# Routing weights stored to DRAM and read back as broadcast rows, in an AdaLN / RWKV / mixture-of-experts kernel

## The chip, the cores and the metric

One core of one Trainium2 chip. The metric is device microseconds of one execution, the median of three runs. TensorE is called PE here, VectorE DVE, ScalarE ACT, GpSimd POOL, and SyncE, which only issues DMAs, SP.

## The reference

`x` is 4 batches of 1024 rows of 256 floats. Cut to what matters:

```
mod = silu(c) @ wmod                      # shifts, scales and gates of each batch
h = layernorm(x) * (1 + ca) + sa
x = x + ga * attn(h)                      # RWKV: projections k, v, r; a scan over time; Wo
h = layernorm(x) * (1 + cb) + sb
logits = h @ gate_w.T                     # 8 experts
topk_vals, topk_idx = top_k(logits, 2);  w = softmax(topk_vals)
comb = zeros((n, 8)).at[rows, topk_idx].add(w)
y = einsum('ne,enh->nh', comb, silu(h @ Wg) * (h @ Wu) @ Wd)     # each expert is 64 wide
y = y + silu(h @ sWg) * (h @ sWu) @ sWd                           # shared expert, 128 wide
x = x + gb * y
```

## The kernel before, in words

The 4096 rows are cut into 8 chunks of 512. Feature data lie transposed: features on the 128 partitions, 512 rows along the free dimension. Software pipelining is written out by hand: each engine has its own function `step(n)` with a fixed order of calls (PE L867, DVE L1222, ACT L547), and in step n it handles four chunks: `before` = n-2 (output of the expert layer), `prev` = n-1 (expert layer), `cur` = n (end of the attention, second norm), `nxt` = n+1 (first norm, projections, scan); DVE also takes the first statistics of `after` = n+2. Steps 0 and 1 have functions of their own, and `step(n)` runs for n = 2 to 9. Steps 2 to 6 have all their chunks; step 7 has no `nxt`, step 8 no `cur`. An engine works through its list strictly in order, and semaphores join the lists.

The expert layer of `prev` in one step: `up(prev, 0..9)` (PE L749) makes the gate and up products of the shared expert (i = 0, 1) and of four expert pairs, six matmuls each. `silu(prev, e)` (ACT L439) waits for `up(2e)`, `gate_up(prev, e)` (DVE L1138) for `up(2e+1)`. `route` (DVE L1080, 19 small operations) makes the routing weights from the logits and writes them to `comb` as a float32r high part and a low part, 16 columns. `turn_comb` (PE L741) transposes them, `comb_out` (ACT L469) copies them to `combT`, and `spread_comb(prev, e)` (PE L789) multiplies `combT` by a selection matrix `sel`, so that a PSUM bank holds the weight of each row on all 64 partitions of its expert. `weigh(prev, e)` (DVE L1150) multiplies by it. `down(prev, oc)` (PE L799) waits for all four `weigh`s and runs 10 matmuls; it is called for oc = 0 and 1.

Beside it in the same step: `turn_attn(cur, k)` (PE L711) transposes the attention output back, `residual1(cur, k)` (DVE L1058) adds x, `stats2(cur)` (DVE L1156) takes its statistics, `rstd` (POOL L296) works out the scale, `normalise2(cur)` (ACT L340, line L331) normalises, and `turn2(cur, kc)` (PE L649, line L631) transposes the result, which waits for all of `normalise2`. `affine2(cur)` (ACT L363), `low_part(cur)` (DVE L1074) and the `up`s of the next step follow. `project(nxt, j)` (PE L659) are the six projections of the next chunk, four matmuls each.

ACT's list ahead of `normalise2(cur)` in each step is: `silu(prev, 4)`, a table load, four exponentials and eight `state_falls`/`output_falls`, `add_bias(nxt, 2)` and `add_bias(nxt, 3)` (L574 to L583).

The end of PE's list in `step(n)` before:

```
up(prev, 6); spread_comb(prev, 1); up(prev, 7); spread_comb(prev, 2)
up(prev, 8); up(prev, 9); spread_comb(prev, 3); spread_comb(prev, 4)
turn_attn(cur, 1); project(nxt, (2, 3, 4))
down(prev, 0); turn2(cur, 0); turn2(cur, 1); project(nxt, (5,)); down(prev, 1)
```

SP (L233) has one in-order list of DMAs: the inputs and weights, then in a loop `load(n + 3)` (waits for `residual1` of chunk n, since `x_in` has three buffers) and `store(n)` (waits for `residual2` of chunk n, which DVE runs in step n+2).

Of the kernel before, what the change touches and what calls it, by code (L numbers as in the profile page):

```python
# [45 lines left out]
def adaln_rwkv_moe(nc, x, Wk, bk, Wv, bv, Wr, br, Wo, bo, tmk, tmv, tmr, time_decay, time_first,  # L46
                   gate_w, Wg, Wu, Wd, sWg, sWu, sWd, cond, wmod, out):
    x_chunks = x.rearrange("b (g t p) h -> (b g) p t h", t=TT, p=P)
    out_chunks = out.rearrange("b (g t p) h -> (b g) p t h", t=TT, p=P)

    with ExitStack() as ctx:
        def sb(name, shape, dt=F32):
# [6 lines left out]
        ident = sb("ident", [P, P])  # L59
        sel = sb("sel", [P, NP, P], F32R)  # L60
        prio = sb("prio", [P, TT, E])
# [39 lines left out]
        r1 = sb("r1", [P, 7, TT])  # L101
        comb = sb("comb", [P, TT, 2 * E], F32R)
        combT = sb("combT", [P, CH], F32R)
        lgT = sb("lgT", [2 * E, CH])
# [14 lines left out]

        sel_f = tmp[0:2 * E, 0, :].rearrange("p (i n) -> p i n", i=NP)  # L120
        rec = arg[:, 0, :, :]
# [7 lines left out]

        comb_bank = {1: cb, 2: cb, 3: cb, 4: tp}  # L130

# [4 lines left out]
        class Norm:  # L136
# [21 lines left out]
            sem(n) for n in ("cond_in", "rows_in", "mod_in", "mod2_in", "up_in", "dn_in", "gw_in"))  # L158
        consts_done, ident_done, sel_done = sem("consts_done"), sem("ident_done"), sem("sel_done")
        zeros_done = sem("zeros_done")  # L160
        sq_in = [sem(f"sq_in{w}") for w in range(4)]
# [44 lines left out]
        combT_done = sem("combT_done")  # L206
        comb_mm = sem("comb_mm")
        up_mm = sem("up_mm")
# [11 lines left out]
        bias_cols = (col["bk"], col["bv"])  # L220
        ROUTE_STEPS = 18
        N_CONSTS2 = 4
# [10 lines left out]
        def _(sp):  # L233
# [28 lines left out]
            load(chunk(2))  # L262
            for n in range(NC - 1):
                if chunk(n + 3):
                    load(chunk(n + 3))
                store(chunk(n))
            last = chunk(NC - 1)
# [10 lines left out]
        def _(pool):  # L278
            nc.gpsimd.memset(ident[:, :], 0.0).then_inc(consts_done, 1)
            nc.gpsimd.memset(sel_f[:, :, :], 0.0).then_inc(consts_done, 1)  # L280
# [3 lines left out]
            pool.wait_ge(consts_done, 5)  # L284
# [3 lines left out]
            for part in range(2):  # L288
                wait(pool, sel_done, part)
                nc.gpsimd.affine_select(  # L290
                    out=sel_f[:, :, :].rearrange("p i (e m) -> p i e m", m=M),
                    in_=sel_f[:, :, :].rearrange("p i (e m) -> p i e m", m=M),
                    compare_op=ALU.not_equal, fill=1.0, base=-E * part,
                    pattern=[[-2, NP], [-1, 2], [0, M]], channel_multiplier=1).then_inc(sel_done, 1)

# [30 lines left out]
        def _(ac):  # L326
# [300 lines left out]
        def _(pe):  # L627
# [112 lines left out]
            @of_chunk  # L740
            def turn_comb(c):  # L741
                pe.wait_ge(comb_done, c.n + 1)
                for t in range(TT):
                    last = nc.tensor.transpose(cb[0:2 * E, t * P:(t + 1) * P], comb[:, t, :].bitcast(F32),  # L744
                                               ident[:, :])
                last.then_inc(comb_turned, 1)

            @of_chunk
            def up(c, i):  # L749
# [36 lines left out]
                last.then_inc(up_mm, 1)  # L786

            @of_chunk
            def spread_comb(c, e):  # L789

                if e == 1:
                    pe.wait_ge(combT_done, c.n + 1)
                elif e < 4:
                    pe.wait_ge(act_done, NP * c.n + e - 1)
                nc.tensor.matmul(comb_bank[e][:, :], sel[:, e - 1, :], combT[:, :], start=True, stop=True  # L795
                                 ).then_inc(comb_mm, 1)

# [37 lines left out]
            def second_step():  # L835
# [31 lines left out]
            def step(n):  # L867
# [85 lines left out]
        def _(ve):  # L953
# [126 lines left out]
            def route(c, first, end):  # L1080
# [5 lines left out]
                for n in range(first, end):  # L1086
# [28 lines left out]
                    elif n == 11:  # L1115
                        ins = V.tensor_tensor(m2, prio[:, :, :], wide(s), ALU.is_equal)
                    elif n == 12:

                        ve.wait_ge(gap_tanh, c.n + 1)
                        ins = V.tensor_scalar(w1, th, -0.5, 0.5, ALU.mult, ALU.add)  # L1120
                    elif n == 13:
                        ins = V.tensor_scalar(w2, th, 0.5, 0.5, ALU.mult, ALU.add)
                    elif n == 14:
                        ins = V.tensor_tensor(w1m, m1, wide(w1), ALU.mult)
                    elif n == 15:
                        ins = V.tensor_tensor(w2m, m2, wide(w2), ALU.mult)
                    elif n == 16:
                        ins = V.tensor_tensor(pr, w1m, w2m, ALU.add)
                    elif n == 17:
                        ins = V.tensor_copy(comb[:, :, 0:E], pr)  # L1130
# [61 lines left out]
            def second_step():  # L1192
# [29 lines left out]
            def step(n):  # L1222
# [41 lines left out]
            nc.vector.memset(hT[0][:, :, 0:1], 0.0)  # L1264

            nc.vector.memset(sel[:, :, :].bitcast(F32), 0.0).then_inc(zeros_done, 1)
            nc.vector.memset(combT[:, :].bitcast(F32), 0.0).then_inc(zeros_done, 1)
            ve.wait_ge(zeros_done, 2)
            ve.wait_ge(sel_done, 2)
            nc.vector.tensor_copy(sel[0:2 * E, :, :], sel_f[:, :, :])  # L1270
            stats1(chunk(0))
# [97 lines left out]
```

## Time and profile before

| | |
|---|---|
| runs | 398.27, 399.09, 398.63 us; median 398.63 us |
| profiled execution | 397.29 us, its span 395.5 us |
| PE busy | 361.1 us, 91% of the span |
| DVE busy | 332.5 us, 84% |
| ACT busy | 295.2 us, 75% |
| POOL busy | 52.2 us, 13% |
| mean granted PE clock | 0.970 of full |
| DMA | 13.28 MB, mean 34 GB/s |

Times in the trace count from the first instruction. Matmuls are pipelined, so the duration of one includes its latency; the distance between the starts of two that follow each other is what one adds. An idle time in brackets stands behind an instruction that its engine waited for, with what released it. The granted clock is in shares of 2.4 GHz.

### The profile page before, as it was taken

Reading aid. Unit: us, or ns where it says so; the run is one execution under the profiler, and the core shown is the slowest. Engines: PE = TensorE matmul, PEld = TensorE weight load, DVE = VectorE, ACT = ScalarE, POOL = GpSimd, SP = SyncE. Lnnn points to the kernel's source line nnn. Section 1 sums busy time; section 2 is a strip of 40 time slices with the busy share of each in tenths; the row PEclk is TensorE's granted clock in tenths of the full one; section 3 lists DMA queues with packets and bytes.
Section 4 is the critical chain, followed back from the end, with each engine's and each line's share of the span. In section 5 each row is a group of like instructions: output and inputs, shape, how many; then the busy total and the mean of one; then the engine's idle time right before and its main releaser. Section 6 shows DMA issues by size and latency. Waiting matters only on the chain.

```text
span 395.5 us, 4302 instructions
## 1 busy us (share of the span) xinstructions
PE 361.1 (91%) x1348; PEld 222.8 (56%) x1348; DVE 332.5 (84%) x666; ACT 295.2 (75%) x467; POOL 52.2 (13%) x74
## 2 busy tenths in 40 slices
PE   4892883999999999999999999999999999979985
PEld 4561332657455745666475746574566546735742
DVE  5799999797999999889998999899998999451731
ACT  2799799766998499948995699849985895336332
POOL 3030024000500042001500070005200200010000
PEclk9995795899999999999999999999999999999999
DMA  8920010000000300002000300030001000100101
GB/s 282 264 81 1 0 53 0 0 2 1 0 1 2 106 1 2 0 33 75 1 2 0 108 0 0 2 106 0 2 1 51 5 0 0 55 0 0 52 4 53
DMA packets 15627, 13.28 MB, mean 34 GB/s; under 512 B 4690, under 2 KB 15092, under 8 KB 15604
## 3 DMA queue, kind: packets, MB, share of 16 engines
q1 hardware_dynamic: 15572, 12.99, 10.7%
q8 instruction: 11, 0.18, 0.2%
q14 instruction: 12, 0.10, 0.1%
q10 hardware_dynamic: 32, 0.01, 0.0%
HBM read 8.80 MB, written 4.19 MB: 33 GB/s over the span
## 4 chain that ended last, share of the span: by engine, by line
PE 79%; DVE 12%; ACT 3%; issue 3%; DMA 1%; POOL 0%; SPq 0%; DVEq 0%; POOLq 0%
PE mm L783 29%; PE mm L679 17%; PE yo L811 15%; PE yo L698 6%; PE yo L707 3%; PE tp L631 3%; DVE mixed L974 2%; DVE n_stats L959 1%; PE cb L795 1%; DVE state L990 1%; ACT n_xn L331 1%; DMA pool_x<-in_L_wmod_dram 1%; DVE state L1009 1%; PE yo L908 1%; PE cb L744 1%
## 5 line engine op out<-in xcount | busy, mean ns | idle before, releaser
L679 PE MATMUL mm<-mixed,WT 128*128 128x512 f32 x192 | 88.4, 603 | 7.1 <-DVE mixed L974 7.1
L811 PE MATMUL yo<-act,w_dn 128*128 128x512 f32 x160 | 71.3, 593 | 3.3 <-DVE act L1153 3.3
L679 PEld LDWEIGHTS mm<-mixed,WT 128*128 128x128 f32 x192 | 36.0, 194 | 48.2 <-issue 39.4
L783 PE MATMUL mm<-h_h,w_up_h 128*128 128x512 f32 x160 | 55.4, 427 | 4.7 <-DVE h_l L1076 3.9
L811 PEld LDWEIGHTS yo<-act,w_dn 128*128 128x128 f32 x160 | 30.1, 190 | 40.4 <-issue 36.4
L783 PE MATMUL mm<-h_h,w_up_l 128*128 128x512 f32 x160 | 50.8, 399 | 0.0
L783 PE MATMUL mm<-h_l,w_up_h 128*128 128x512 f32 x160 | 50.7, 398 | 0.0
L303 POOL TENSOR_TENSOR n_ve<-n_mv,small 128x4 f32<-128x4 f32 x16 | 9.3, 581 | 297.6 <-DVE n_mv L963 297.6
L441 ACT ACTIVATE pool_g<-mm 128x512 f32<-128x512 f32 x40 | 23.5, 588 | 24.2 <-PE mm L783 24.2
L974 DVE SCALAR_TENSOR_TENSOR mixed<-hT,cols,mixed 128x512 f32<-128x512 f32 x48 | 33.7, 744 | 2.4 <-ACT mixed L390 2.4
L379 ACT ACTIVATE kv<-mm,cols 128x512 f32<-128x512 f32 x32 | 21.7, 678 | 18.0 <-PE mm L679 18.0
L783 PEld LDWEIGHTS mm<-h_l,w_up_h 128*128 128x128 f32 x160 | 30.3, 190 | 7.4
L783 PEld LDWEIGHTS mm<-h_h,w_up_l 128*128 128x128 f32 x160 | 30.3, 190 | 7.4
L783 PEld LDWEIGHTS mm<-h_h,w_up_h 128*128 128x128 f32 x160 | 27.6, 191 | 11.3 <-DVE h_l L1076 4.8
L390 ACT ACTIVATE mixed<-hT,rest 128x512 f32<-128x512 f32 x48 | 30.9, 710 | 0.0
L698 PE MATMUL yo<-pool_n,WT 128*128 128x512 f32 x64 | 29.6, 592 | 0.0
L306 POOL TENSOR_TENSOR n_rstd<-n_ve,small 128x4 f32<-128x4 f32 x16 | 24.4, 1524 | 1.3
L1146 DVE TENSOR_TENSOR pool_g<-mm,pool_g 128x512 f32<-128x512 f32 x32 | 21.8, 684 | 3.1 <-PE mm L783 2.6
L1153 DVE TENSOR_TENSOR act<-cb,pool_g 128x512 f32<-128x512 f32 x24 | 16.5, 686 | 8.7 <-PE cb L795 8.7
L631 PE MATMUL tp<-ident,n_xn 128*128 128x128 f32 x88 | 15.2, 302 | 8.2 <-ACT n_xn L331 8.1
L631 PEld LDWEIGHTS tp<-ident,n_xn 128*128 128x128 f32 x88 | 11.9, 155 | 17.7 <-ACT n_xn L331 11.9
L990 DVE TENSOR_TENSOR_SCAN state<-decay,state,kv 128x512 f32<-128x512 f32 x16 | 20.5, 1281 | 0.8 <-ACT kv L379 0.6
(152 smaller groups left out, 654.2 us busy)
## 6 DMA issues: line engine op xcount, KB each, us to landing
x_in<-in_L_attn_x_dram SPq DMA_DIRECT2D x8, 512.0 KB, 4.6
out_dram<-pool_x SPq DMA_DIRECT2D x5, 512.0 KB, 3.1
pool_x<-in_L_wmod_dram SPq DMA_DIRECT2D x2, 512.0 KB, 5.4
out_dram<-x_third SPq DMA_DIRECT2D x2, 512.0 KB, 3.0
pool_x<-in_L_wmod_dram SPq DMA_DIRECT2D x2, 256.0 KB, 3.8
pool_g<-in_L_ffn_Wg_dram SPq DMA_DIRECT2D x2, 256.0 KB, 4.9
pool_g<-in_L_ffn_Wu_dram SPq DMA_DIRECT2D x2, 256.0 KB, 4.2
w_dn<-in_L_ffn_Wd_dram SPq DMA_DIRECT2D x1, 512.0 KB, 4.2
```

What stands on the lines that cost most here:

```text
L306: nc.gpsimd.tensor_tensor(norm.rstd[:, :], norm.ve[:, :], small[:, 1, :], ALU.pow).then_inc(norm.rstd_done if direct else norm.pool_step, 1)
L379: nc.scalar.activation(kv[:, w, kc, :], mm[PROJECT_BANK[j]][:, :], ACT.Identity, bias=bias_cols[w][:, kc:kc + 1]).then_inc(kv_done, 1)
L390: nc.scalar.activation(mixed[:, w, kc, :], hT[c.half][:, kc, 0:CH], ACT.Identity, scale=rest[:, KH * w + kc:KH * w + kc + 1]).then_inc(par ...
L441: nc.scalar.activation(sg[:, e, :], mm[UP_BANK[2 * e]][:, :], ACT.Silu).then_inc(silu_done, 1)
L631: last = nc.tensor.transpose(dst[:, t * P:(t + 1) * P], norm.xn[:, t, kc * P:(kc + 1) * P], ident[:, :])
L679: last = nc.tensor.matmul(mm[PROJECT_BANK[j]][:, :], WT[:, w, kc, oc * P:(oc + 1) * P], mixed[:, w, kc, :], start=(kc == 0), stop=(kc == K ...
L698: last = nc.tensor.matmul(yo[oc][:, :], WT[:, O, kc, oc * P:(oc + 1) * P], rw[:, kc, :], start=(kc == 0), stop=(kc == KH - 1))
L783: last = nc.tensor.matmul(mm[UP_BANK[i]][:, :], w[:, kc, gu, e * P:(e + 1) * P], rhs[:, kc, :], start=(n == 0), stop=(n == 3 * KH - 1))
L811: last = nc.tensor.matmul(yo[oc][:, :], w_dn[:, e, oc * P:(oc + 1) * P], act[:, e, :], start=(e == 0), stop=(e == NB - 1))
L974: nc.vector.scalar_tensor_tensor(out=mixed[:, w, kc, :], in0=hT[c.half][:, kc, 1:CH + 1], scalar=mix_cols[w][:, kc:kc + 1], in1=mixed[:, w ...
L990: nc.vector.tensor_tensor_scan(state[:, 0, h, 1:CH + 1], decay[:, h:h + 1].to_broadcast([P, CH]), kv[:, K, h, :], state[:, 0, h, 0:1], ALU ...
L1146: nc.vector.tensor_tensor(dst[:, e, :], mm[UP_BANK[2 * e + 1]][:, :], sg[:, e, :], ALU.mult).then_inc(prod_done, 1)
```

## The change

The selection matrix, its set-up and the four `spread_comb` matmuls of a chunk go, and with them the split of the weights in two parts (two of 19 `route` operations). `combT` (8 x 512) is stored to a DRAM tensor, and SP reads it back in eight DMAs, each one row onto 64 partitions (128 KB written), into `weights`, from which `weigh` reads. On SP, `spread(prev)` stands behind `store(before)`, and the load behind it is that of chunk n+4 of its loop index. In `step(n)` PE runs all four remaining projections and `turn2(cur, 0)` ahead of `down(prev, 0)`, and `turn2(cur, 1)` between the two `down`s; DVE runs the four `weigh`s behind `stats2`. ACT's list keeps its order; `comb_out` gets a wait for the last store of `combT`.

```
@@ SP
+            def spread(c):
+                sp.wait_ge(combT_done, c.n + 1)
+                sp.dma_start(comb_dram, combT[:, :]).then_inc(comb_stored, 16)
+                sp.wait_ge(comb_stored, 16 * (c.n + 1))
+                for i in range(NP):
+                    wait(sp, act_done, NP * (c.n - 1) + i + 1)
+                    for e in range(2):
+                        sp.dma_start(weights[e * M:(e + 1) * M, i, :],
+                                     comb_dram[2 * i + e:2 * i + e + 1, :].to_broadcast([M, CH])
+                                     ).then_inc(spread_in[i], 16)
...
-            for n in range(NC - 1):
-                if chunk(n + 3):
-                    load(chunk(n + 3))
-                store(chunk(n))
+            load(chunk(3))
+            for n in range(NC):
+                if n:
+                    store(chunk(n - 1))
+                spread(chunk(n))
+                if chunk(n + 4):
+                    load(chunk(n + 4))
@@ ACT comb_out
+                wait(ac, comb_stored, 16 * c.n)
-                nc.scalar.activation(combT[0:2 * E, :], cb[0:2 * E, :], ACT.Identity).then_inc(combT_done, 1)
+                nc.scalar.activation(combT[:, :], cb[0:E, :], ACT.Identity).then_inc(combT_done, 1)
@@ PE turn2
-                    pe.wait_ge(act_done, NP * c.n - kc)
+                    pe.wait_ge(combT_done, c.n)
@@ PE second_step
-                spread_comb(prev, 1)
...
-                spread_comb(prev, 4)
@@ PE step
                 up(prev, 6)
-                spread_comb(prev, 1)
                 up(prev, 7)
-                spread_comb(prev, 2)
                 up(prev, 8)
                 up(prev, 9)
-                spread_comb(prev, 3)
-                spread_comb(prev, 4)
                 turn_attn(cur, 1)
-                project(nxt, (2, 3, 4))
+                project(nxt, (2, 3, 4, 5))
+                turn2(cur, 0)
                 down(prev, 0)
-                turn2(cur, 0)
                 turn2(cur, 1)
-                project(nxt, (5,))
                 down(prev, 1)
@@ DVE weigh
-                ve.wait_ge(comb_mm, NP * c.n + e)
+                ve.wait_ge(spread_in[e - 1], 32 * (c.n + 1))
...
-                nc.vector.tensor_tensor(act[:, e, :], comb_bank[e][:, :], sg[:, e, :], ALU.mult).then_inc(act_done, 1)
+                nc.vector.tensor_tensor(act[:, e, :], weights[:, e - 1, :], sg[:, e, :], ALU.mult).then_inc(act_done, 1)
@@ DVE step
                 gate_up(prev, 2)
-                weigh(prev, 1)
                 scan_max(nxt, 1)
-                weigh(prev, 2)
                 gate_up(prev, 3)
                 residual1(cur, 0)
                 gate_up(prev, 4)
+                residual1(cur, 1)
+                stats2(cur)
+                weigh(prev, 1)
+                weigh(prev, 2)
                 weigh(prev, 3)
-                residual1(cur, 1)
                 weigh(prev, 4)
-                stats2(cur)
```

## Rows read from the trace of the kernel before

**Rows 1.** Windows of two steps: busy us of each engine, PE's clock, DMA.

```profile
241.60:284.20 42.60, 42.60 (x162) 26.02 (x161) 40.01 (x80) 35.61 (x59) 7.05 (x8) 1.00 0.08 25
326.50:361.50 35.00, 32.05 (x130) 20.69 (x128) 20.39 (x48) 16.30 (x25) 1.61 (x4) 1.00 0.05 15
```

**Rows 2.** Timeline of PE at the end of step 5: start, us, engine, line.

```profile
267.07 0.39 PE L795 MATMUL tp<-combT,sel 128*128 128x512 f32 x1
267.30 0.60 PE L707 MATMUL yo<-ident,oT 128*128 128x128 f32 x4
267.74 5.32 PE L679 MATMUL mm<-mixed,WT 128*128 128x512 f32 x12
272.89 4.45 PE L811 MATMUL yo<-act,w_dn 128*128 128x512 f32 x10
277.18 0.60 PE L631 MATMUL tp<-ident,n_xn 128*128 128x128 f32 x4
...
284.07 0.60 PE L631 MATMUL tp<-ident,n_xn 128*128 128x128 f32 x4
```

**Rows 3.** Timeline of ACT in the same stretch.

```profile
260.53 0.59 ACT L471 ACTIVATE combT<-cb 16x512 fp32r<-16x512 f32 x1 [2.02 <-PE cb L744]
...
265.64 0.60 ACT L441 ACTIVATE pool_g<-mm 128x512 f32<-128x512 f32 x1 [1.45 <-PE mm L783]
...
274.46 2.06 ACT L331 ACTIVATE n_xn<-x_third,n_shift,n_rstd 128x256 f32<-128x256 f32 x4
...
280.97 2.08 ACT L331 ACTIVATE n_xn<-x_in,n_shift,n_rstd 128x256 f32<-128x256 f32 x4
```

**Rows 4.** Timeline of DVE in the same stretch.

```profile
267.11 0.69 DVE L1146 TENSOR_TENSOR pool_g<-mm,pool_g 128x512 f32<-128x512 f32 x1
...
269.51 1.39 DVE L959 BATCH_NORM_STATS2 n_stats<-x_third 128x6 f32<-128x256 f32 x4
...
282.23 1.22 DVE L1076 TENSOR_TENSOR h_l<-pool_x,h_h 128x1024 fp32r<-128x1024 f32 x1
```

**Rows 5.** Timeline of SP: one store in step 5, the longest issue at the start.

```profile
11.29 2.55 SPq L259 DMA_DIRECT2D pool_g<-in_L_ffn_sWu_dram  x1
...
261.40 0.38 SPq L240 DMA_DIRECT2D out_dram<-pool_x  x1
```

**Rows 6.** DMA issues of the page: KB each, median us to landing.

```profile
x_in<-in_L_attn_x_dram SPq DMA_DIRECT2D x8, 512.0 KB, 4.6
out_dram<-pool_x SPq DMA_DIRECT2D x5, 512.0 KB, 3.1
...
out_dram<-pool_x SPq DMA_DIRECT2D x2, 256.0 KB, 2.2
```

**Rows 7.** Timeline of step 7, PE and DVE.

```profile
350.66 4.56 PE L811 MATMUL yo<-act,w_dn 128*128 128x512 f32 x10 [1.75 <-DVE act L1153]
356.42 0.66 PE L631 MATMUL tp<-ident,n_xn 128*128 128x128 f32 x4 [1.20 <-ACT n_xn L331]
...
350.53 1.39 DVE L959 BATCH_NORM_STATS2 n_stats<-pool_x 128x6 f32<-128x256 f32 x4
```

**Rows 8.** Timeline of step 8, ACT, SP and PE.

```profile
373.04 0.59 ACT L471 ACTIVATE combT<-cb 16x512 fp32r<-16x512 f32 x1 [2.11 <-PE cb L744]
...
373.32 0.37 SPq L240 DMA_DIRECT2D out_dram<-pool_x  x1
...
381.11 8.85 PE L811 MATMUL yo<-act,w_dn 128*128 128x512 f32 x20 [1.58 <-DVE act L1153]
```

**Rows 9.** PE in step 0, and windows there: PE busy, clock, DMA.

```profile
61.96 1.12 PE L631 MATMUL tp<-ident,n_xn 128*128 128x128 f32 x4 [3.54 <-ACT n_xn L331]
...
67.78 1.22 PE L783 MATMUL mm<-h_h,w_up_h 128*128 128x512 f32 x2 [3.85 <-DVE h_l L1076]
...
60.00:62.00 2.00, 0.04 (x1) 0.77 0.00 0
...
70.00:72.00 2.00, 2.00 (x9) 0.67 0.00 0
```

More of the change, by code:

```diff
@@ L49, in adaln_rwkv_moe @@
     out_chunks = out.rearrange("b (g t p) h -> (b g) p t h", t=TT, p=P)
+    comb_dram = nc.dram_tensor("comb_dram", (E, CH), F32, kind="Internal").ap()
     with ExitStack() as ctx:
@@ L59, in adaln_rwkv_moe @@
         ident = sb("ident", [P, P])
-        sel = sb("sel", [P, NP, P], F32R)
         prio = sb("prio", [P, TT, E])
@@ L101, in adaln_rwkv_moe @@
         r1 = sb("r1", [P, 7, TT])
-        comb = sb("comb", [P, TT, 2 * E], F32R)
-        combT = sb("combT", [P, CH], F32R)
+        comb = sb("comb", [P, TT, E])
+        combT = sb("combT", [E, CH])
+        weights = sb("weights", [P, NP, CH])
         lgT = sb("lgT", [2 * E, CH])
@@ L118, in adaln_rwkv_moe @@
         sg = pool_g[:, :].rearrange("p (e n) -> p e n", e=NB)
-        sel_f = tmp[0:2 * E, 0, :].rearrange("p (i n) -> p i n", i=NP)
         rec = arg[:, 0, :, :]
@@ L128, in adaln_rwkv_moe @@
         cb = ctx.enter_context(nc.psum_tensor("cb", [P, CH], F32))
-        comb_bank = {1: cb, 2: cb, 3: cb, 4: tp}
         UP_BANK = (0, 1, 2, 3, 0, 3, 0, 1, 2, 0)
@@ L158, in adaln_rwkv_moe @@
             sem(n) for n in ("cond_in", "rows_in", "mod_in", "mod2_in", "up_in", "dn_in", "gw_in"))
-        consts_done, ident_done, sel_done = sem("consts_done"), sem("ident_done"), sem("sel_done")
-        zeros_done = sem("zeros_done")
+        consts_done, ident_done = sem("consts_done"), sem("ident_done")
         sq_in = [sem(f"sq_in{w}") for w in range(4)]
@@ L206, in adaln_rwkv_moe @@
         combT_done = sem("combT_done")
-        comb_mm = sem("comb_mm")
+        comb_stored = sem("comb_stored")
+        spread_in = [sem(f"spread_in{i}") for i in range(NP)]
         up_mm = sem("up_mm")
@@ L220, in adaln_rwkv_moe @@
         bias_cols = (col["bk"], col["bv"])
-        ROUTE_STEPS = 18
+        ROUTE_STEPS = 16
         N_CONSTS2 = 4
@@ L279, in _ @@
             nc.gpsimd.memset(ident[:, :], 0.0).then_inc(consts_done, 1)
-            nc.gpsimd.memset(sel_f[:, :, :], 0.0).then_inc(consts_done, 1)
             nc.gpsimd.memset(small[:, 0, :], EPS).then_inc(consts_done, 1)
@@ L283, in _ @@
             nc.gpsimd.memset(small[:, 2, :], 0.0).then_inc(consts_done, 1)
-            pool.wait_ge(consts_done, 5)
+            pool.wait_ge(consts_done, 4)
             nc.gpsimd.affine_select(out=ident[:, :], in_=ident[:, :], compare_op=ALU.not_equal, fill=1.0,
                                     base=0, pattern=[[-1, P]], channel_multiplier=1).then_inc(ident_done, 1)
[L288 to L294, printed above, removed]
             def rstd(norm, c):
@@ L743, in turn_comb @@
                 for t in range(TT):
-                    last = nc.tensor.transpose(cb[0:2 * E, t * P:(t + 1) * P], comb[:, t, :].bitcast(F32),
-                                               ident[:, :])
+                    last = nc.tensor.transpose(cb[0:E, t * P:(t + 1) * P], comb[:, t, :], ident[:, :])
                 last.then_inc(comb_turned, 1)
@@ L786, in up @@
                 last.then_inc(up_mm, 1)
[L788 to L796, printed above, removed]
             @of_chunk
@@ L887, in step @@
                 up(prev, 6)
-                spread_comb(prev, 1)
                 up(prev, 7)
-                spread_comb(prev, 2)
                 up(prev, 8)
                 up(prev, 9)
-                spread_comb(prev, 3)
-                spread_comb(prev, 4)
                 turn_attn(cur, 1)
-                project(nxt, (2, 3, 4))
+                project(nxt, (2, 3, 4, 5))
+                turn2(cur, 0)
                 down(prev, 0)
-                turn2(cur, 0)
                 turn2(cur, 1)
-                project(nxt, (5,))
                 down(prev, 1)
@@ L1126, in route @@
                         ins = V.tensor_tensor(w2m, m2, wide(w2), ALU.mult)
[L1127 to L1130, printed above, removed]
-                    else:
-                        V.tensor_tensor(comb[:, :, E:2 * E], pr, comb[:, :, 0:E].bitcast(F32), ALU.subtract
-                                        ).then_inc(comb_done, 1)
+                    else:
+                        V.tensor_tensor(comb[:, :, :], w1m, w2m, ALU.add).then_inc(comb_done, 1)
                         return
@@ L1243, in step @@
                 gate_up(prev, 2)
-                weigh(prev, 1)
                 scan_max(nxt, 1)
-                weigh(prev, 2)
                 gate_up(prev, 3)
@@ L1249, in step @@
                 gate_up(prev, 4)
+                residual1(cur, 1)
+                stats2(cur)
+                weigh(prev, 1)
+                weigh(prev, 2)
                 weigh(prev, 3)
-                residual1(cur, 1)
                 weigh(prev, 4)
-                stats2(cur)
                 stats1(after)
@@ L1264, in _ @@
             nc.vector.memset(hT[0][:, :, 0:1], 0.0)
[L1266 to L1270, printed above, removed]
             stats1(chunk(0))
```

## The prediction

> **What bounds the kernel now.** First the windows of whole steps: in a full step of 42.6 us PE is busy for all of it at full clock, while DVE has 2.6 us to spare and ACT 7.0; step 7 is another matter, PE is idle there for 3 us [rows 1]. So in steps 2 to 6 time is what PE executes, as long as nobody makes it wait. Then the timelines, to see how near the next waits are. PE's end of step 5 is closed: `turn_attn`, three projections, `down`, two `turn2` at 277.18, project 5, `down`, and step 6 begins at 284.07 [rows 2]. The row to keep in mind is ACT's: `normalise2` runs from 274.46 to 276.52, with no idle time before it, in a chain without a gap from `silu(prev, 4)` at 265.64 on [rows 3]. PE's `turn2` comes 0.66 us after its end. That is all the slack between the two, and `down(prev, 0)` stands in PE's list ahead of it and covers the wait.
>
> **What goes.** A `spread_comb` matmul shows 0.39 us, but the next instruction starts 0.23 after it (267.07 to 267.30) [rows 2]: four are 0.92 us a chunk, eight chunks 7.4. The transposes of `comb` still stream the same 128 columns; I take nothing for their eight rows fewer. Two small `route` operations less help DVE, which is not the bound. The selection matrix's set-up lies beside the input loads: nothing. The loads "two steps ahead" too: three `x_in` buffers exist already, and no full step shows a wait for one, since PE has no idle time in them [rows 1].
>
> **What is moved.** In `step(n)`, `turn2(cur, 0)` now stands ahead of `down(prev, 0)`, behind all projections. I work it out in the times of step 5.
> - Two `spread_comb`s ahead of `up(prev, 8)` are gone, so ACT's chain starts 0.46 earlier, and its order is unchanged: `normalise2` ends at 276.52 - 0.46 = 276.06. In step 0 the transpose starts 0.05 or so behind such an end: 276.11.
> - POOL does not decide it: in step 7, where nothing else holds ACT, `turn2` starts 5.89 us after `stats2` [rows 7], so `normalise2` 3.8 after it. Here `stats2`, at 269.51 before [rows 4], comes one `weigh` (0.6) and the 0.46 earlier, and its scale is ready at 272.3, while ACT's chain gets there at 274.0.
> - PE gets there at 267.74 - 0.92 = 266.82 plus four projections. Three take 272.89 - 267.74 = 5.15, so four take 6.87: 273.69 [rows 2].
> - PE therefore stands idle for 276.11 - 273.69 = 2.42 us, where before it was executing `down`.
> - What remains is `turn2` 0.44, `down` 4.29 (272.89 to 277.18), `turn2` 0.44, `down` 4.29: the end is at 285.57 against 284.07. Each full step is **1.5 us longer**; five of them, 7.5.
>
> Does the late part hold? `affine2(cur, 1)` now waits for a `turn2` that ends near 281.3, 1.5 us of ACT follow, and `normalise1`, which started at 280.97 and takes 2.08 [rows 3], ends at 285.0, ahead of 285.57. `low_part`, at 282.23 before [rows 4], starts at 283 and ends 1.2 later, before the next `up`. Neither adds.
>
> **The weights' way round DRAM** is what is added. `comb_out` ends at 261.12 [rows 3]. SP is behind the 512 KB store issued at 261.40 [rows 5], so the small store goes out at 261.8. No row shows 16 KB landing; the ends are 2.2 us from its issue (the 256 KB stores) and the 3.1 of the store ahead of it plus 2.2 [rows 6]. I take 0.2 behind the big store, 264.7, since it is small and next in the same queue. Eight issues follow at about 0.45 each (0.38 for a plain store, 2.55 at worst in the crowded start [rows 5]): the last goes out at 267.9. A 128 KB load lands after at least 2.2 and at most 4.6 us (512 KB) [rows 6]; I take 2.5, so the last is there at 270.4. DVE reaches the last `weigh` near 271.4: `gate_up` 4 at 267.11 - 0.46, `residual1` and 1.8 of statistics, then three `weigh`s of 0.6 [rows 4]. So nothing waits. What is queued behind a late `weigh` on DVE is the scans of `nxt`, whose sums are ready just ahead of `low_part`, at 282.2, and are asked for by ACT at 285.0, so a landing up to 274 costs nothing either. The cover is thus PE's own new wait; without it `down` would want the weights at 273.7.
>
> **Other steps.** Step 1 keeps `turn2` behind `down(prev, 0)`: only -0.92. Step 7 has no projections. There `down` filled most of the wait for `normalise2` (`stats2` at 350.53, `turn2` 5.89 later at 356.42 [rows 7]). Now `stats2` comes 0.46 and two `weigh`s (1.2) earlier, at 348.87, `turn2` at 354.76, and both `down`s lie behind it: the second starts at 354.76 + 0.5 + 4.29 + 0.43 = 359.98, where it was 357.35 (356.42 + 0.93). That is +2.6. PE was last busy at 350.66 - 1.75 - 0.92 = 347.99 [rows 7], so it is idle for 6.8 us. In step 0 the clock had fallen to 1.2 GHz by the end of an idle stretch of 3.54 us and stayed there from the resumption at 67.78 to about 71.3 (0.67 is the mean of 70 to 72), 3.5 us that do the work of 1.77 [rows 9]. I add 1.8 for that: **+4.4**.
>
> Step 8 has neither projections nor `turn2`: `down` waits for the weights alone. `comb_out` ends at 373.63, the store of 512 KB goes out at 373.32 [rows 8] and lands at 376.4, the small one at 376.6, the last load is issued at 379.8 and lands at 382.3; with `weigh`, `down` starts at 383.05 against 381.11 [rows 8]: +1.9. PE is idle 4.4 us before it, so 1.8 of low clock again: **+3.7**.
>
> The Trainium skill, "DMA: Bandwidth & Descriptors", Anatomy of one DMA, gives about 2.0 us fixed for a DMA plus its bytes at 436 GB/s. Taken by that the small store lands at 375.8, the last load at 381.3, and step 8 would cost 1 us less; no row here shows a DMA so small.
>
> **Sum**: -0.92 + 7.5 + 4.4 + 3.7 = +14.7 us. On the profiled execution's own 397.29 that is 412.0. It lies 1.3 under the median of the runs, 398.63, and from there the sum gives **413**.
>
> **The rivals.**
> - *The clock falls in every full step.* In step 0 PE had been idle for 2.66 us when it fell (idle from 58.42, and 0.77 as the mean of 60 to 62 puts the fall at 61.08) [rows 9]; gaps of 1.75 and 1.20 us in step 7 left it full [rows 1, 7]. My gap of 2.42 lies between, nearer the first. At 1.77 each, five more falls are +8.9: 422. Against it: dense matmuls lie on both sides of the gap.
> - *The weights are late.* Loads that take 1 us each to issue and 4.6 to land are there at 276.3 (264.7 + 7 + 4.6), 2.3 past the point from which `weigh` passes its delay on to the reciprocal and the next step. Five steps are 11.5, and in step 8 the last is there at 388.2 instead of 382.3: 17 more, 430. For it: each reads one DRAM row 64 times, which no row shows. Against it: the queue is empty then but for one store.
> - *Faster.* `turn2` finds `normalise2` done, so that the gap does not open, and the eight times 0.92 come through: 391. It would need ACT's chain to be 2.4 us shorter from `silu(prev, 4)` on. It decides in one place, ACT at 276.1 against PE at 273.7, and nothing in the diff shortens that list.
> - *The change does little*: the stall is as long as what is saved, 398 to 399. It needs a gap of 0.9 instead of 2.42 and no cost at the end.
>
> **How the numbers follow.** Forecast 0.66, falling clock 0.13 (partly: it may fall in some steps), late weights 0.11, faster 0.06, little change 0.04. A measurement of this kernel tells about 0.2%, 0.8 us. The forecast without low clock in steps 7 and 8 and with the shorter DMAs is 413 - 3.6 - 1 = 408.5, a little more off each step's 1.5 gives 406; upward the falling clock reaches 421. Faster 0.07, same 0.03, slower 0.90.
>
> **What would show it.** PE's share in a full step falls from 100% to 95%, with an idle of about 2.4 us before L631, released by ACT's n_xn, in steps 2 to 6, and steps of 44.2 us. No wait of DVE for `weights` in those steps; one in step 8. A PE gap of nearly 7 us in step 7, with the clock at half behind it. I am wrong if `turn2` does not wait (the order of ACT was misread), if DVE waits long for the DMAs, or if the clock falls each step.

## The result, and the profile after

The changed kernel takes **418.23 us** (median of 4 runs, 416.80 to 419.44) against 398.45 (398.22 to 399.09) for the kernel before in the same session: a ratio of 1.0492, interval 1.0454 to 1.0531. The forecast was 413, the range 406 to 421: side and range were right, and the size was 5 us short. The profiled execution took 418.83, its span is 417.0 against 395.5.

From the page: busy time and clock, the chain that ended last, and the loads that are new.

```profile
PE 362.0 (87%) x1316; PEld 219.4 (53%) x1316; DVE 329.6 (79%) x647; ACT 295.9 (71%) x467; POOL 47.7 (11%) x71
...
PEclk9995795999999999999999999999999999779969
...
PE 63%; ACT 18%; DVE 10%; issue 3%; DMA 3%; POOL 1%; SPq 0%; DVEq 0%; POOLq 0%; ACTq 0%
...
weights<-comb_dram SPq DMA_DIRECT2D x64, 128.0 KB, 3.0
```

All engines have about as much work as before; PE, at 361.1 us then, even a little more, though 32 matmuls went: those that run at half clock in steps 7 and 8 take longer. What grew is idle time. PE's share of the last chain, 79% before, is 63%, and ACT's went from 3% to 18%. The clock digits are lower at three places: early in the kernel, where they were low before, and at two places near the end, slices 35 and 36 and slice 39, which are steps 7 and 8.

The step lengths say where the time went. They are taken from the start of the router's product in one step to the same in the next, in the two profiled executions:

| | before | after | change | predicted |
|---|---|---|---|---|
| up to the first router product | 72.74 | 74.95 | +2.2 | 0 |
| step 1 | 42.50 | 42.04 | -0.5 | -0.92 |
| steps 2 to 6 | 212.91 (42.67, 42.66, 42.67, 42.67, 42.24) | 220.75 (44.24, 44.23, 44.23, 44.25, 43.80) | +7.8 | +7.5 |
| step 7 | 34.91 | 41.18 | +6.3 | +4.4 |
| step 8 to the last matmul's end | 28.78 | 34.40 | +5.6 | +3.7 |
| sum | | | +21.5 | +14.7 |

PE's timeline: step 1, the end of step 5 (answers to [rows 2]), steps 7 and 8 (to [rows 7, 8]).

```profile
115.48 0.73 PE L791 MATMUL mm<-h_h,w_up_h 128*128 128x512 f32 x2 [0.86 <-DVE h_l L1065]
...
273.27 7.03 PE L688 MATMUL mm<-mixed,WT 128*128 128x512 f32 x16
282.57 0.66 PE L639 MATMUL tp<-ident,n_xn 128*128 128x128 f32 x4 [2.27 <-ACT n_xn L338]
283.07 4.46 PE L809 MATMUL yo<-act,w_dn 128*128 128x512 f32 x10
287.36 0.60 PE L639 MATMUL cb<-ident,n_xn 128*128 128x128 f32 x4
...
365.36 1.12 PE L639 MATMUL tp<-ident,n_xn 128*128 128x128 f32 x4 [7.76 <-ACT n_xn L338]
366.27 6.68 PE L809 MATMUL yo<-act,w_dn 128*128 128x512 f32 x10
...
400.40 11.05 PE L809 MATMUL yo<-act,w_dn 128*128 128x512 f32 x20 [5.94 <-DVE act L1137]
```

The row at 282.57 is the forecast's main row. The bracket counts from the modelled end of the last projection, which holds 0.16 us of latency (a 512-column matmul shows 0.39 and its successor starts after 0.23 [rows 2]), so the hole in PE's stream is 2.27 + 0.16 = 2.43 us, where 2.42 was forecast. It is there in each of steps 2 to 6, with 2.27 each time. `down` takes 4.46 us at full clock in step 5 and 6.68 in step 7.

ACT's timeline in step 5 (to [rows 3]), and its `comb_out` in step 8.

```profile
271.63 0.60 ACT L448 ACTIVATE pool_g<-mm 128x512 f32<-128x512 f32 x1 [0.98 <-PE mm L791]
...
280.45 2.07 ACT L338 ACTIVATE n_xn<-x_third,n_shift,n_rstd 128x256 f32<-128x256 f32 x4
...
388.90 0.59 ACT L479 ACTIVATE combT<-cb 8x512 f32<-8x512 f32 x1 [2.11 <-PE cb L753]
```

ACT is busy without a break from `silu(prev, 4)` at 271.63 to the end of `normalise2` at 282.52, and `turn2` starts 0.05 behind that end.

DVE's timeline in step 3, in step 5 (to [rows 4]), in step 7 and in step 8.

```profile
190.75 0.69 DVE L1137 TENSOR_TENSOR act<-weights,pool_g 128x512 f32<-128x512 f32 x1 [1.12 <-DMA weights<-comb_dram]
...
273.10 0.69 DVE L1130 TENSOR_TENSOR pool_g<-mm,pool_g 128x512 f32<-128x512 f32 x1 [1.51 <-PE mm L791]
...
276.23 1.86 DVE L1137 TENSOR_TENSOR act<-weights,pool_g 128x512 f32<-128x512 f32 x3
278.38 0.69 DVE L1137 TENSOR_TENSOR act<-weights,pool_g 128x512 f32<-128x512 f32 x1 [0.29 <-DMA weights<-comb_dram]
...
358.66 1.41 DVE L948 BATCH_NORM_STATS2 n_stats<-pool_x 128x6 f32<-128x256 f32 x4
...
360.40 2.46 DVE L1137 TENSOR_TENSOR act<-weights,pool_g 128x512 f32<-128x512 f32 x4
...
399.65 0.69 DVE L1137 TENSOR_TENSOR act<-weights,pool_g 128x512 f32<-128x512 f32 x1 [0.30 <-DMA weights<-comb_dram]
```

SP's timeline, the same steps (to [rows 5, 8]).

```profile
267.42 0.38 SPq L240 DMA_DIRECT2D out_dram<-pool_x  x1
267.84 0.41 SPq L246 DMA_DIRECT2D comb_dram<-combT  x1
270.88 5.04 SPq L251 DMA_DIRECT2D weights<-comb_dram  x8
...
392.37 4.92 SPq L251 DMA_DIRECT2D weights<-comb_dram  x8
```

The small store takes 3.04 us to come back (267.84 to 270.88; 2.75 to 2.77 in the other steps that have a big store ahead of it), and each of the eight issues 0.63 us. The last weight in step 5 is there at 278.38, 0.29 us later than DVE asks for it, and nothing behind it in that step is late. In steps 2 and 3 DVE waits longer for it, 0.85 and 1.12 us, and those steps take 44.24 and 44.23 us like the others.

### The profile page after: what moved, and what is told of

It is laid out like the page before. It is cut to its first block, busy times and chain, and to the rows that moved or that the text cites. A ratio compares the mean times of both kernels' runs of the same rounds, so it can differ in the third digit from the quotient of the medians.

```text
span 417.0 us, 4299 instructions
## 1 busy us (share of the span) xinstructions
PE 362.0 (87%) x1316; PEld 219.4 (53%) x1316; DVE 329.6 (79%) x647; ACT 295.9 (71%) x467; POOL 47.7 (11%) x71
## 4 chain that ended last, share of the span: by engine, by line
PE 63%; ACT 18%; DVE 10%; issue 3%; DMA 3%; POOL 1%; SPq 0%; DVEq 0%; POOLq 0%; ACTq 0%
PE mm L791 24%; PE yo L809 16%; PE mm L688 7%; PE yo L707 7%; ACT arg L403 5%; ACT n_xn L338 3%; ACT arg L417 3%; PE tp L639 3%; PE yo L716 2%; ACT kv L386 2%; ACT L584 2%; DMA weights<-comb_dram 1%; DVE n_stats L948 1%; DMA pool_x<-in_L_wmod_dram 1%; DVE mixed L963 1%
## 5 line engine op out<-in xcount | busy, mean ns | idle before, releaser
L688 PE MATMUL mm<-mixed,WT 128*128 128x512 f32 x192 | 89.7, 615 | 6.8 <-DVE mixed L963 6.8
L809 PE MATMUL yo<-act,w_dn 128*128 128x512 f32 x160 | 75.7, 623 | 5.9 <-DVE act L1137 5.9
L688 PEld LDWEIGHTS mm<-mixed,WT 128*128 128x128 f32 x192 | 37.3, 198 | 51.6 <-issue 43.4
L809 PEld LDWEIGHTS yo<-act,w_dn 128*128 128x128 f32 x160 | 31.1, 202 | 40.7 <-issue 34.3
L448 ACT ACTIVATE pool_g<-mm 128x512 f32<-128x512 f32 x40 | 23.5, 588 | 20.7 <-PE mm L791 20.7
L791 PEld LDWEIGHTS mm<-h_h,w_up_h 128*128 128x128 f32 x160 | 27.7, 192 | 11.9 <-DVE h_l L1065 5.3
L313 POOL TENSOR_TENSOR n_rstd<-n_ve,small 128x4 f32<-128x4 f32 x16 | 25.3, 1580 | 1.2
L1137 DVE TENSOR_TENSOR act<-weights,pool_g 128x512 f32<-128x512 f32 x32 | 20.5, 681 | 4.7 <-DMA weights<-comb_dram 4.6
```

The source lines that it names most:

```text
L313: nc.gpsimd.tensor_tensor(norm.rstd[:, :], norm.ve[:, :], small[:, 1, :], ALU.pow).then_inc(norm.rstd_done if direct else norm.pool_step, 1)
L448: nc.scalar.activation(sg[:, e, :], mm[UP_BANK[2 * e]][:, :], ACT.Silu).then_inc(silu_done, 1)
L688: last = nc.tensor.matmul(mm[PROJECT_BANK[j]][:, :], WT[:, w, kc, oc * P:(oc + 1) * P], mixed[:, w, kc, :], start=(kc == 0), stop=(kc == K ...
L791: last = nc.tensor.matmul(mm[UP_BANK[i]][:, :], w[:, kc, gu, e * P:(e + 1) * P], rhs[:, kc, :], start=(n == 0), stop=(n == 3 * KH - 1))
L809: last = nc.tensor.matmul(yo[oc][:, :], w_dn[:, e, oc * P:(oc + 1) * P], act[:, e, :], start=(e == 0), stop=(e == NB - 1))
```

## The experiments

Each ratio is to the kernel before, run in the same session on the same chip (medians 399.25, 399.09 and 399.44 us in the three sessions). "After" is the changed kernel.

**1. The order of PE alone.** Two kernels that cross: after with the old order of PE's `step(n)`, and before with the new one.

```
 turn_attn(cur, 1)
-project(nxt, (2, 3, 4, 5))
-turn2(cur, 0)
+project(nxt, (2, 3, 4))
 down(prev, 0)
+turn2(cur, 0)
 turn2(cur, 1)
+project(nxt, (5,))
 down(prev, 1)
```

This is the edit of the first; the second has its reverse, applied to the kernel before.

> The changed kernel with one edit: PE's list in step(n) has the order of the kernel before again (three projections, down 0, both turn2, the last projection, down 1). My theory: the waiting of turn2 for normalise2 is what costs in the full steps (2.27 us of idle PE in each). Here down(prev, 0) covers it again; the weights are multiplied 31.1 us into the step and down 0 wants them at about 30.6, so each full step is 42.2 to 42.5 us instead of 44.23, step 7 loses about 5 of its surplus, the surplus of 5.6 us in step 8 stays: 403 to 407 us, about 0.97 of the changed kernel. Rival, the way round DRAM is what costs in the full steps: 417 to 419, as the changed kernel.

> The kernel before with one edit: PE's list in step(n) has the order of the changed kernel (four projections, turn2 0, down 0, turn2 1, down 1); the selection products and DVE's order stay. My theory: PE reaches turn2 at 28.4 minus 0 (33.2 us into a full step) and normalise2 ends at 35.1, so a gap of about 1.9 us and steps of 44.6 us, five times 1.9 is 9.7, and step 7 pays 4 to 6 with the low clock behind its gap: 411 to 415 us. Rival, the order is free and the DRAM path costs: 398 to 399.

Measured: after with the old order 408.33 us, ratio 1.0227 (1.0189 to 1.0265); before with the new order 416.33 us, 1.0443 (1.0397 to 1.0489). PE, then POOL, of the second:

```profile
283.67 0.66 PE L631 MATMUL tp<-ident,n_xn 128*128 128x128 f32 x4 [1.81 <-ACT n_xn L331]
...
367.69 1.11 PE L631 MATMUL tp<-ident,n_xn 128*128 128x128 f32 x4 [7.50 <-ACT n_xn L331]
```

```profile
363.69 0.20 POOL L303 TENSOR_TENSOR n_ve<-n_mv,small 128x4 f32<-128x4 f32 x1 [37.38 <-DVE n_mv L962]
363.97 1.01 POOL L306 TENSOR_TENSOR n_rstd<-n_ve,small 128x4 f32<-128x4 f32 x1
```

What follows: the order of PE's calls, with not one DMA added, gives 17.1 of the 19.8 us. Steps 2 to 6 of that kernel are 10.2 us longer than before's and step 7 6.9, while its step 8 is before's (28.76). The gap is shown to come from PE's order alone, made by moving two calls, `project(nxt, 5)` and `turn2(cur, 0)`, ahead of `down(prev, 0)`. Taken out of after, the same order gives back only 9.9 us (418.23 to 408.33): the two parts of the change do not simply add. With the old order in place, steps 2 to 6 of the first kernel are 1.0 us longer than before's, step 7 3.4 and step 8 5.3. Both results were 1.3 us above their expected ranges. In the first kernel, with the gap gone, full steps should have been 42.67 - 0.92 = 41.75 us, and steps 2 to 5 are 42.75 to 43.68 (step 6 is 41.73, where before's is 42.24). Something else had become the bound. PE of that kernel shows two small waits in a step, neither of them for ACT:

```profile
275.88 4.56 PE L809 MATMUL yo<-act,w_dn 128*128 128x512 f32 x10 [0.33 <-DVE act L1138]
288.04 0.73 PE L791 MATMUL mm<-h_h,w_up_h 128*128 128x512 f32 x2 [0.28 <-DVE h_l L1066]
```

**2. The length of ACT's list.** In after, `normalise2(cur)` ahead of an exponential and an `add_bias`.

```
 output_falls(nxt)
+normalise2(cur)
 state_exponentials(nxt, 1)
 add_bias(nxt, 3)
-normalise2(cur)
```

> The changed kernel with one edit: in ACT's list of step(n) normalise2(cur) stands ahead of state_exponentials(nxt, 1) and add_bias(nxt, 3), which take 1.14 and 0.57 us. My theory (ACT's list is what turn2 waits for): normalise2 ends 1.6 us earlier, the gap of PE falls from 2.27 to about 0.7 us, full steps from 44.23 to 42.6, five of them: 409 to 411 us. Rival (the statistics and POOL's scale are what it waits for): no change, 417 to 419.

Measured: 411.46 us, 1.0315 (1.0279 to 1.0352). Full steps are 42.74 to 43.78, the gap 0.78 to 1.32 us. ACT's timeline shows why not less:

```profile
275.94 2.07 ACT L338 ACTIVATE n_xn<-x_third,n_shift,n_rstd 128x256 f32<-128x256 f32 x4 [0.56 <-POOL n_shift L321]
```

What follows: the time is 6.8 us under after's, just above the 409 to 411 that was expected, without touching PE or the DMAs. Steps 2 to 6 hold 4.8 of it (215.93 us against 220.75), so it is ACT's position in its list that the gap measures. Steps 7 and 8 are 1.2 and 0.6 us shorter, and that is not the edit's: PE waits there as long as in after (7.76 and 5.87 us, against 7.76 and 5.94), but stayed at half clock for 3.0 and 3.3 us instead of 5.4 and 4.5. 0.56 us on, POOL's scale is what is late next.

**3. The DRAM route.** Two kernels with SP's `spread` ahead of the 512 KB store: one in the kernel of part 1 with the old order of PE, one in after.

```
+spread(chunk(n))
 if n:
     store(chunk(n - 1))
-spread(chunk(n))
```

> As e1_old_pe_order, and on SP spread(prev) stands ahead of store(before), so that the small store is not behind the 512 KB one. The small store landed 1.5 us after its issue in step 1, where nothing was ahead of it, against 2.75 in the other steps, and it is issued 0.4 us earlier. My theory: the weights come 1.6 us earlier, down 0 no longer waits (about 0.5 us less in each of five steps), and step 8 is 1.6 us shorter: 2.5 to 5 us less than e1_old_pe_order. Rival (it is the eight loads alone that make them late): as e1_old_pe_order.

> The changed kernel with one edit: on SP spread(prev) stands ahead of store(before). PE's order is that of the changed kernel. Theory: the full steps do not ask for the weights so early, the gap before turn2 stays at 2.2 to 2.3 us and the steps at 44.2, and only step 8 gains, 1.5 to 2 us: 416 to 417. Rival (the weights' way round DRAM sets the full steps too): 1.6 us less in each, 408 to 410.

Measured: the first 406.73 us, 1.0192 (1.0162 to 1.0222); the second 417.59 us, 1.0470 (1.0449 to 1.0492). SP of the first, then PE of the second:

```profile
261.94 0.29 SPq L246 DMA_DIRECT2D comb_dram<-combT  x1
263.41 5.16 SPq L251 DMA_DIRECT2D weights<-comb_dram  x8
268.61 0.59 SPq L240 DMA_DIRECT2D out_dram<-pool_x  x1
```

```profile
281.49 0.66 PE L639 MATMUL tp<-ident,n_xn 128*128 128x128 f32 x4 [2.27 <-ACT n_xn L338]
```

What follows: without the big store ahead of it the small one comes back after 1.47 us, not 3.04. In after, where this brings the loads 1.8 us forward in step 5 (from 21.2 us behind the router product to 19.4), it changes no full step: the gap is 2.27 us as before the edit, the steps 44.23. The rival "late weights" falls, since weights that come so much earlier ought to have shortened them. Only step 8's gap fell, from 5.94 to 4.72, and the time is 0.6 us above the 416 to 417 that was expected. In the kernel with the old PE order the gain was 1.6 us of medians, less than the 2.5 to 5 expected. Of its full steps only step 3 gained much, from 43.68 to 42.73: there DVE had waited 0.88 us for the last weights. Steps 2, 4 and 5 stayed at 42.7 (42.75 to 42.87 before the edit) with no wait of DVE for the weights left. So the DMAs were not what kept these from 41.75. DVE's timeline of that kernel names it:

```profile
267.44 0.69 DVE L1131 TENSOR_TENSOR pool_g<-mm,pool_g 128x512 f32<-128x512 f32 x1 [1.51 <-PE mm L791]
```

All four `weigh`s now stand behind `stats2`, so DVE has nothing to do while it waits for the last `up`: 1.51 us here and 0.40 before the `gate_up` ahead. DVE works 40.39 us in a step of after; with 1.9 of such waits it is at 42.3, near the 42.7 that the step takes.

**4. DVE's order.** As the kernel with `spread` first and the old PE order, with `stats1(after)` moved from behind the `weigh`s into that wait.

```
 residual1(cur, 0)
+stats1(after)
 gate_up(prev, 4)
...
 weigh(prev, 4)
-stats1(after)
```

> As e4_spread_first, and in DVE's list of step(n) stats1(after), which waits for nothing here, stands between residual1(cur, 0) and gate_up(prev, 4), where e4_spread_first shows DVE idle for 1.51 us in each full step. Theory: with PE's order back, what holds the full steps at 42.7 us instead of the 41.75 that PE executes is DVE, whose weigh calls all stand behind stats2 and no longer fill its waits for the up products; with 1.5 us of its work moved there, down 0 and the next up no longer wait for it: steps of 41.8 to 42.0, 4 us less than e4_spread_first, 402 to 403.5 us. Rival, the weights themselves are late or PE has another bound: no change, 406 to 407.

Measured: 405.03 us, 1.0149 (1.0125 to 1.0173). Full steps are 42.27 (step 3 is 42.74, where DVE waits 0.37 us for the weights, and step 6 is 41.75); the wait for `h_l` is gone, one is left on PE:

```profile
273.92 4.56 PE L809 MATMUL yo<-act,w_dn 128*128 128x512 f32 x10 [0.27 <-DVE act L1138]
```

What follows: filling DVE's wait takes 0.45 us off steps 2, 4 and 5, 1.3 us in all, though DVE does the same work. That its order was a cost of its own is shown. The time is 1.5 us above the top of what was expected: full steps did not reach 41.75, and steps 7 and 8 are still long, 37.84 and 33.2 us. The edit has nothing to shorten them. They are 1.1 and 0.7 us under those of part 3's kernel all the same, and in step 7 that is the clock alone. `down` waits 5.32 us in both kernels and starts at 353.66 and 353.94; windows of PE, part 3's kernel and then this one:

```profile
358.00:360.00 2.00, 2.00 (x4) 0.66 0.00 0
```

```profile
356.00:358.00 2.00, 2.00 (x5) 0.65 0.00 0
```

By these means the half clock lasted to 359.4 in the one, 5.7 us, and to 357.4 in the other, 3.5 us. So about 1 us in a difference between two of these kernels can be the clock's in each of steps 7 and 8, and a claim on an edit has to be read from the steps.

**5. The route only where there is cover.** The kernel of part 4 for chunks 0 to 5, and before's selection products for chunks 6 and 7, whose `down`s have no projections beside them.

```
+K0 = NC - 2
 def spread_comb(c, e):
+    if c.n < K0:
+        return
...
+if n < K0:
+    spread(chunk(n))
```

> As e5_stats1_moved for chunks 0 to 5; chunks 6 and 7 get their weights by the selection products of the kernel before, with DVE's order of before in their steps. Theory: the rest of the surplus lies in steps 7 and 8, where no projections cover the way round DRAM (38.95 - 34.91 = 4.0 us in step 7 and 5.1 from there to the end in e4_spread_first, the low clock behind the two gaps included), and is gone here: 392 to 396 us, faster than the kernel before by 1%, from what the selection products cost in five full steps. Rival, the surplus in the last steps has another cause: 400 to 403.

Measured: **396.86 us**, 0.9951 (0.9931 to 0.9971). Steps 2 to 5 take 42.27 us, step 6 41.74, steps 7 and 8 34.90 and 28.77, as before's (34.91, 28.78), with before's waits:

```profile
350.38 4.56 PE L842 MATMUL yo<-act,w_dn 128*128 128x512 f32 x10 [1.75 <-DVE act L1193]
...
380.81 4.56 PE L842 MATMUL yo<-act,w_dn 128*128 128x512 f32 x10 [1.58 <-DVE act L1193]
```

What follows: with both orders mended and the last two chunks left as they were, the change is worth 0.5%. That is half of what was expected, and the time is 0.9 us above the 392 to 396: the full steps still hold the wait of 0.27 us for the last `weigh`. The losses of steps 7 and 8 belong to the DRAM route and what was ordered for it.

**6. Half as many loads.** The kernel with `spread` first and the old PE order, each pair of rows in one DMA onto all 128 partitions.

```
-for e in range(2):
-    sp.dma_start(weights[e * M:(e + 1) * M, i, :],
-                 comb_dram[2 * i + e:2 * i + e + 1, :].to_broadcast([M, CH])
+sp.dma_start(weights[:, i, :],
+             comb_dram[2 * i:2 * i + 2, :].unsqueeze(1).to_broadcast([2, M, CH])
```

> As e4_spread_first, with the weights read back in four DMAs of 128 partitions instead of eight of 64. If SP's 0.62 us per issue is a cost per DMA, the last load is issued after 1.9 instead of 4.3 us, lands 2.4 us earlier, and step 8 is up to 2.4 us shorter: 404 to 405 us. If it goes by the number of descriptors or partitions, an issue takes 1.2 us and nothing changes: 406 to 407.

Measured: 533.10 us, 1.3363 (1.3334 to 1.3393), where 404 to 407 was expected. A window of two us in the middle of the loads, in this kernel and in after (all engines; the last three columns are PE's clock, the DMA share and GB/s), and DVE's timeline of this kernel:

```profile
275.00:277.00 2.00, 2.00 (x8) 1.04 (x7) 1.90 (x4) 1.99 (x4) 0.00 (x0) 1.00 0.13 50
```

```profile
275.00:277.00 2.00, 2.00 (x6) 0.94 (x5) 1.96 (x10) 2.00 (x4) 0.56 (x1) 1.00 0.68 221
```

```profile
283.89 0.69 DVE L1137 TENSOR_TENSOR act<-weights,pool_g 128x512 f32<-128x512 f32 x1 [4.57 <-DMA weights<-comb_dram]
```

What follows: a share of 0.13 is what 2 of the 16 DMA engines make when they are busy all the time, and 0.68 as much as 11 of them. Where the pattern begins with the dimension of 2, the same bytes went at 50 GB/s instead of 221. DVE waits 4.4 to 5 us for each of the last three, and PE 15 us in each of steps 2 to 6. The Trainium skill, "DMA: Bandwidth & Descriptors", Why a DMA increments its semaphore by 16 and not by 1, says that a DMA is divided over the largest number of engines up to 16 that divides the slowest dimension of both patterns that is larger than 1; this trace agrees, with a share of 2 of 16.

**7. A wait that was taken too early.** `down` waits for all four `weigh`s before its first matmul. Here, in the kernel of part 5 and in before, it waits for each one only ahead of the matmul that reads it.

```
 if oc == 0:
-    pe.wait_ge(act_done, NP * (c.n + 1))
-    pe.wait_ge(prod_done, NB * (c.n + 1))
+    pe.wait_ge(prod_done, NB * c.n + 1)
 for e in range(NB):
+    if oc == 0 and e:
+        pe.wait_ge(act_done, NP * c.n + e)
```

> As e6_hybrid, and down(prev, 0) waits for each weigh just ahead of the two matmuls that read it, instead of for all four at its start. e6_hybrid's full steps are 42.27 us where PE executes 41.75, with PE waiting 0.27 us for the last weigh ahead of down 0. Theory: that wait is the rest, steps become 41.75 to 41.9 us, and the 1.75 and 1.58 us of waiting ahead of down in steps 7 and 8 nearly go: 396.9 - 2 - 3 = 391 to 393 us. Rival: DVE is as busy as before and the wait only moves to the next step's up (h2_l): 394 to 396.

> The kernel before with the same edit to down(prev, 0), the control for e9_hybrid_staged_down. Its full steps have no idle PE, so only the 1.75 and 1.58 us ahead of down in steps 7 and 8 can go, of which step 7 gives some back to its wait for normalise2 (1.20 us now): 396 to 398 us, 1.5 to 3 less than before.

Measured: the first **394.72 us**, 0.9896 (0.9864 to 0.9929); the second 396.74 us, 0.9954 (0.9917 to 0.9991). The second is as expected, the first 1.7 us above its range and inside its rival's. The rival's mechanism, a wait that only moves to the next `up`, is not what happened. The full steps of the first are 41.74, before's less the whole 0.93: PE has no wait left there. Step 8 is 26.9 in both, 1.9 less than before. Step 7 is 34.90 in the second and 36.31 in the first, and that is the clock. PE and windows of PE in the first, then in the second:

```profile
353.55 1.11 PE L658 MATMUL tp<-ident,n_xn 128*128 128x128 f32 x4 [3.21 <-ACT n_xn L354]
```

```profile
352.00:354.00 2.00, 0.45 (x2) 0.75 0.00 0
354.00:356.00 2.00, 2.00 (x9) 0.50 0.03 8
```

```profile
358.87 0.66 PE L631 MATMUL tp<-ident,n_xn 128*128 128x128 f32 x4 [3.21 <-ACT n_xn L331]
```

```profile
359.00:361.00 2.00, 2.00 (x11) 1.00 0.03 8
```

What follows: the version of part 5 with this edit beats both kernels, before by a ratio of 1.0% (4.7 us of medians) and after by 23.5 us of medians; of the 4.7, the kernel before has 2.7 to gain by this edit alone. The other 2.0 are what the DRAM route is worth with its orders mended. The intervals of the two ratios overlap, so the times alone hardly show it; the steps do, with 4.7 us less in steps 2 to 6 (208.24 against 212.91) and 1.4 lost again to the clock in step 7. The earlier `down` moved the idle time of step 7 from two waits of 1.75 and 1.20 us to one of 3.21, and step 7 gained nothing from it, since `turn2` still waits for `normalise2`. In the first kernel the clock had fallen by 353.0 (0.75 is the mean of 352 to 354), 2.7 us into the idle stretch.

## Why the prediction came out as it did

**Right: the gap in the full steps.** Forecast 2.42 us of idle PE, a step of 44.2 and 7.5 in all; measured 2.43, 44.23 and 7.8. ACT's place in its list, PE's place and the length of the four projections were all read rightly from [rows 2, 3], and parts 1 and 2 show that order on either side opens and closes the gap. The clock stayed at 1.00 through all five gaps, so the rival "the clock falls in every full step" did not happen. Nor did the weights delay a full step of after (part 3), although DVE waits for the last of them in steps 2, 3 and 5, 0.85, 1.12 and 0.29 us, where the forecast had no wait. One reading was wrong without effect: by the diff two `weigh`s, not one, no longer stand ahead of `stats2`, so POOL's scale was due at 271.7, not 272.3. ACT's chain came later in either case.

**Mis-sized: the price of the loads.** The prediction took 0.45 us an issue and 2.5 to land. Rows show 0.63 and a median of 3.0. In step 8 the last load was there at 399.65, 10.2 us after `comb_out`'s end (388.90 + 0.59), where the prediction had 8.7. That is 1.5 of the 1.9 us that step 8's term lacked; the rest is the clock's, next. The sum that stood beside it from the Trainium skill, "DMA: Bandwidth & Descriptors", Anatomy of one DMA, is given there for the path of GpSimd's DMAs, and these are SP's. It was too short for the loads (2.3 us, measured 2.7 to 4.1) and too long for the small store alone (2.0 us, measured 1.47 in part 3).

**Mis-sized: the time at half clock.** The prediction took 3.5 us at 1.2 GHz after a resumption, 1.8 us lost, from [rows 9]. Windows of after's PE (PE busy, clock, DMA share, GB/s) in steps 7 and 8:

```profile
370.00:372.00 2.00, 2.00 (x5) 0.82 0.00 0
...
404.00:406.00 2.00, 2.00 (x5) 0.78 0.00 0
```

A mean of 0.82 puts the rise 0.7 us into the first window: 365.36 to 370.7 at half clock, 5.4 us, 2.7 lost. The second puts it 0.9 us in: 400.40 to 404.9, 4.5 us, 2.2 lost. Together 1.3 us more than forecast. Part of that is chance: the forecast rested on one sample, and in steps 7 and 8 of the kernels of parts 1 to 4 the stretch is anything from 3.0 to 5.8 us, also where the waits ahead of it are equally long. What sets it no run shows.

**Missed: POOL beside DVE.** The prediction took 5.89 us from `stats2` to `turn2` in step 7 from [rows 7]. It was 365.36 - 358.66 = 6.70. There DVE stood idle behind `stats2`; now it runs the four `weigh`s, and POOL needs longer for the scale, 2.64 us from its first operation to the end of its last (360.56 to 363.20), whose first two are:

```profile
360.56 0.56 POOL L310 TENSOR_TENSOR n_ve<-n_mv,small 128x4 f32<-128x4 f32 x1 [36.86 <-DVE n_mv L952]
361.20 1.33 POOL L313 TENSOR_TENSOR n_rstd<-n_ve,small 128x4 f32<-128x4 f32 x1
```

The kernel with the new PE order alone, which leaves DVE idle there, has 0.20 and 1.01 for the same two (part 1) and 5.88 for the whole. The Trainium skill, "SBUF — State Buffer", Who interferes with whom, says that a DVE operation with both inputs in SBUF contends with a GpSimd operation that reads SBUF; the `weigh`s have both there since the change, and the trace agrees, with 0.8 us over the chain. That it is this contention is the page's reading, but before's own step 5 supports it. Beside DVE's statistics, which read one tensor, the same two POOL operations took 0.20 and 1.01 us (271.40 to 272.69); beside DVE's scans, with `arg` and `state` both in SBUF, they took:

```profile
273.62 1.18 POOL L303 TENSOR_TENSOR n_ve<-n_mv,small 128x4 f32<-128x4 f32 x1
274.87 1.90 POOL L306 TENSOR_TENSOR n_rstd<-n_ve,small 128x4 f32<-128x4 f32 x1
```

So it is not enough that DVE is busy; what it reads matters. With 0.8 for POOL, 0.9 for the clock and 0.2 for a `stats2` that came 1.46 us sooner behind the router product than before, not 1.66, step 7's 1.9 is accounted for.

**Missed: DVE as the next bound.** The prediction gave step 1 the full -0.92 and, in its "faster" rival, every step. Step 1 got -0.5, because PE waits 0.86 us for `h_l` at 115.48. In full steps the gap hid it; with the gap gone the order of DVE's list holds them at 42.7 (parts 3 and 4). The failing step is "Two small `route` operations less help DVE, which is not the bound": DVE had 2.6 us to spare [rows 1], and the same change that shortens PE's list by 0.92 makes DVE wait 1.9 us for the `up`s with nothing to fill it. This is why the rival at 391 was too low even without the gap: it needed DVE's list mended too, and `down`'s early wait. Only with both (part 7) are the full steps shorter by the whole 0.93.

**Chance: the start.** The first router product came 2.2 us later in the profiled execution. It is between 73.8 and 75.3 in the profiles of the two experiments that leave before's set-up as it is, and 72.7 in before, so this much comes and goes without an edit. Without it the steps add up to +19.3, and the medians differ by 19.8.

## What to carry over

A long operation that stands in a list between a producer on another engine and its consumer is cover, even if nothing names it so: before moving a call, ask what each engine was doing while it would have waited, in both directions (PE covering ACT, `weigh` covering DVE). Then look at the steps without the usual neighbours, the last ones above all: 11.9 of the 21.5 us came from two of them. Compare kernels step by step: up to 1.8 us between two of them was the length of a stretch at half clock, which no edit had touched. And wait for each operand where it is read, not once for all of them: worth 0.5% in the old kernel, for four lines.

## What was not expected of the hardware

- A DMA whose pattern begins with a dimension of 2 ran on 2 of 16 DMA engines, at 50 GB/s against 221 (part 6), and made the kernel 31% longer than the one with eight loads (533.10 to 406.73). 512 KB stores beside it landed after 15.4 us, not 3.0.
- An idle stretch of 3.21 us let PE's clock fall to 1.2 GHz in one kernel of part 7 and left it at 2.4 in the other, with the same work ahead of it; it had fallen after 2.66 us in [rows 9]. Five gaps of 2.27 us never did it. What it cost where it fell also differs, and the idle time does not set it: 5.4 us at half clock after 7.76 idle in after and 3.0 after the same 7.76 in part 2; after 5.32 idle, 4.4 in part 1's first kernel, 5.7 in part 3's and 3.5 in part 4's.
- A store of 16 KB holds up what depends on it for 1.47 us by itself and for 2.75 to 3.04 behind a 512 KB store on the same queue.
- POOL's 128x4 operations took 0.20 and 1.01 us beside idle DVE or its statistics, 0.56 and 1.33 beside the `weigh`s from SBUF, and 1.18 and 1.90 beside DVE's scans.
